# A one-core transformer tower: two layer norms share one power on GpSimd, and small operations go from GpSimd to VectorE

## The chip, the core and the metric

The kernel runs on one core of a Trainium2 chip. The metric is the device time of one execution in microseconds, the median of several runs. The core's engines are TensorE (PE, with its weight loads PEld), VectorE (DVE), ScalarE (ACT), GpSimd (POOL) and SyncE (SP), which only issues DMAs here.

## The reference

For 128 sequences of 128 tokens, three parts follow each other; D is 64.

```python
# embedding: gather, three gelus, one fused gelu, first norm
item_emb, geo, visit = emb_table[ids], geo_table[ids], visit_table[ids]
cat = concat(gelu(item_emb @ w_item + b), gelu(geo @ w_geo + b), gelu(visit @ w_visit + b))
h = item_emb + 0.1 * layer_norm(gelu(cat @ w_fuse + b_fuse), gamma, beta) * (ids != 0)
# attention, 4 heads of 16, on the second norm of h
h = h + attention(layernorm(h))
# feed-forward on the third norm x3; of each sequence's 128 tokens 63 are routed
x3 = layernorm(h)
weights = x3 @ wr + br
y = gelu_tanh(x3 @ w1 + b1) @ w2 + b2
h = h + x3 + where(selected, y * weights, 0)
```

The routing takes the 63 tokens of highest weight of each sequence. The kernel computes y for all tokens and applies the selection at the end. Each norm needs (variance + 1e-5) ** -0.5 for each token.

## The kernel before

Tokens of a sequence lie on the 128 partitions, sequences on the free axis. The 128 sequences are worked in 32 groups of four (`GB` is 4). Every engine runs the same software pipeline written by hand: a function `step(i, odd, half)` of each engine is called for i from -2 to 33, and in it a is group i+2 (embedding and first norm), b is i+1 (second norm, q, k, v), c is i (scores and softmax), e is i-1 (values and output projection) and d is i-2 (third norm and feed-forward). GpSimd's step also fetches group i+3. The first and last steps are written out; those between are a hardware loop of two steps a turn. `on(g)` says whether group g exists. Each engine works its own instructions in order and waits on semaphores counted by group.

What the change and the prediction touch:

- Each norm has statistics (`stats`, L573), an aggregation into mean and variance (`moments`, L580, tiles `mv1` to `mv3`), the reciprocal square root `rs1` to `rs3` (`rstd` on GpSimd: L352 adds epsilon, L355 is the power with `minus_half`), and a normalization on VectorE (`normalize`, L585, into `x2` and `x3`). All of `mv`, `rs` have four columns, one for each sequence of the group.
- For the first norm GpSimd multiplies `rs1` by the mask `valid` (L412); VectorE uses it in L761, which writes the state `R` (h1) from `t1`, `rs1` and `u`.
- `fetch` on GpSimd copies four columns of indices (L338) into `idx` and starts four gathers (L344) into `G`. `visit` (L373) and `base` (L361, L366) prepare the gathered rows.
- L417 and L420 on GpSimd multiply x3 by the routing weights and add x3 to R.
- L669 on VectorE takes a sequence's maximum of the scores; there are four in a step. TensorE transposes them (L961) when all are there. TensorE also transposes x2 (L953) and x3 (L980).
- L678 adds the output projection (TensorE L827) to R; TensorE waits for it in L924 of the same step.
- ScalarE's second gelu `hid` (L520) and the softmax's exponential (L527) each need a table load, as does the first gelu (L471). L478 copies the values' product and stands once in a step.

Of the kernel before, what the change touches and what calls it, by code (L numbers as in the profile page):

```python
# [32 lines left out]
ALU = mybir.AluOpType  # L33
# [11 lines left out]
GB = 4  # L45
# [33 lines left out]
def build(nc, ids, table, packed, out):  # L79
    with ExitStack() as ctx:  # L80
# [3 lines left out]
        def sem(name):  # L84
# [33 lines left out]
        rs1, rs2, rs3 = (sb(f"rs{n}", [P, GB]) for n in (1, 2, 3))  # L118
        minus_half = sb("minus_half", [P, GB])
# [53 lines left out]
            "st1_ready", "mv1_ready", "rs1_ready", "rm1_ready", "t1_ready",  # L173
            "u0_ready", "u_ready", "h1_ready", "st2_ready", "mv2_ready", "rs2_ready", "x2_ready",
# [4 lines left out]
            "h2_ready", "st3_ready", "mv3_ready", "rs3_ready", "x3_ready",   # L179
# [155 lines left out]
        def _(pool):  # L335
            def fetch(g, par):

                pool.tensor_copy(idx[par][:, :], of(idx_all, g)).then_inc(S["idx_ready"], 1)  # L338
# [64 lines left out]
            def step(i, odd, half):  # L403
                a, d, nxt = i + 2, i - 2, i + 3
                if on(d):
                    rstd(mv3, rs3, "mv3_ready", "rs3_ready", d)
                if on(nxt):
                    fetch(nxt, 1 - odd)
                if on(a):
                    rstd(mv1, rs1, "mv1_ready", "rs1_ready", a)  # L410
                    wait(pool, "rs1_ready", 2, a, alone=True)
                    pool.tensor_tensor(rs1[:, :], rs1[:, :], of(valid, a), ALU.mult  # L412
                                       ).then_inc(S["rm1_ready"], 1)
                if on(d):
# [10 lines left out]
                if on(a):  # L425
                    rstd(mv2, rs2, "mv2_ready", "rs2_ready", a)
# [110 lines left out]
        def _(dve):  # L537
# [6 lines left out]

            dve.memset(ones_r[:, :].bitcast(F32), 1.0)
            dve.wait_ge(consts_in, 16)
# [29 lines left out]
            def moments(st, mv, st_done, mv_done, g):  # L576
# [4 lines left out]
                last.then_inc(S[mv_done], 1)  # L581

# [90 lines left out]
            def step(i, odd, half):  # L673
                a, b, c, e, d = i + 2, i + 1, i, i - 1, i - 2
                if on(d):
# [5 lines left out]
                if on(b):  # L681
                    moments(st2, mv2, "st2_ready", "mv2_ready", b)
                if on(d):
                    wait(dve, "h2_ready", 1, d, alone=True)
                    stats(kept(d), st3, "st3_ready", d)
                if on(c):
                    maxima(c, (0,))
                if on(d):
                    moments(st3, mv3, "st3_ready", "mv3_ready", d)
# [4 lines left out]
                if on(b):  # L694

                    wait(dve, "rs2_ready", 2, b)
# [6 lines left out]
                if on(d):  # L703
                    wait(dve, "rs3_ready", 2, d)
# [33 lines left out]
                if on(a):  # L738

                    moments(st1, mv1, "st1_ready", "mv1_ready", a)  # L740
                    wait(dve, "mv1_ready", 1, a)
# [13 lines left out]
                if on(a):  # L755
# [3 lines left out]
                    wait(dve, "rm1_ready", 1, a)  # L759
                    for s in range(GB):  # L760
                        last = dve.scalar_tensor_tensor(kept(a)(s), t1[:, s, :], rs1[:, s:s + 1],  # L761
# [24 lines left out]
            pipeline(dve, step)  # L786
# [307 lines left out]
```

## Time and profile before

| | |
|---|---|
| median of 3 runs | 580.38 us (578.63 to 581.15) |
| profiled execution | 582.28 us, span 580.5 us |
| PE busy | 488.0 us, 84% |
| VectorE busy | 444.6 us, 77% |
| ScalarE busy | 411.6 us, 71% |
| GpSimd busy | 378.0 us, 65% |
| TensorE's granted clock, mean | 0.942 of full |

The span runs from the first to the last instruction. Busy is the time in which an engine has an instruction in work. The chain of waits is followed back from the last instruction, at each step to what released it.

### The profile page before, as it was taken

Reading aid. Unit: us, or ns where it says so; the run is one execution under the profiler, and the core shown is the slowest. Engines: PE = TensorE matmul, PEld = TensorE weight load, DVE = VectorE, ACT = ScalarE, POOL = GpSimd, SP = SyncE. Lnnn points to the kernel's source line nnn. Section 1 sums busy time; section 2 is a strip of 40 time slices with the busy share of each in tenths; the row PEclk is TensorE's granted clock in tenths of the full one; section 3 lists DMA queues with packets and bytes.
Section 4 is the critical chain, followed back from the end, with each engine's and each line's share of the span. In section 5 each row is a group of like instructions: output and inputs, shape, how many; then the busy total and the mean of one; then the engine's idle time right before and its main releaser. Section 6 shows DMA issues by size and latency. Waiting matters only on the chain.

```text
span 580.5 us, 14228 instructions
## 1 busy us (share of the span) xinstructions
PE 488.0 (84%) x4100; PEld 377.4 (65%) x4100; DVE 444.6 (77%) x1757; ACT 411.6 (71%) x694; POOL 378.0 (65%) x571
## 2 busy tenths in 40 slices
PE   0767788988999899898999999899998897988644
PEld 0445566767777677776777777677776765765443
DVE  5266667887888888778878888788887884887887
ACT  1326676788888788787787888788887774866730
POOL 6576456666777677667767677767776674442575
PEclk9879889999999999899999999999999997999855
DMA  3154444544454544545444444445454443333344
GB/s 99 21 94 114 100 104 82 101 105 106 108 110 109 112 106 103 111 90 112 99 95 100 106 105 109 107 107 112 112 107 99 99 100 66 90 92 91 76 102 116
DMA packets 89634, 57.74 MB, mean 99 GB/s; under 512 B 27408, under 2 KB 79248, under 8 KB 89488
## 3 DMA queue, kind: packets, MB, share of 16 engines
q1 hardware_dynamic: 83472, 47.55, 33.0%
q0 software_dynamic: 6144, 9.97, 11.8%
q8 instruction: 8, 0.13, 0.1%
q14 instruction: 10, 0.08, 0.1%
HBM read 11.08 MB, written 4.19 MB: 26 GB/s over the span
## 4 chain that ended last, share of the span: by engine, by line
PE 40%; ACT 16%; issue 14%; DVE 11%; POOL 9%; another core or an unknown queue 6%; DMA 2%; ACTq 0%; SPq 0%; DVEq 0%; POOLq 0%
PE psum L924 5%; POOL G L344 4%; PE psum L917 4%; PE psum L861 4%; PE psum L945 4%; ACT L520 3%; POOL rs L355 3%; PE psum L968 3%; ACT L527 3%; PE psum L943 3%; PE psum L1003 3%; PE psum L897 3%; PE psum L837 2%; PE psum L931 2%
## 5 line engine op out<-in xcount | busy, mean ns | idle before, releaser
L344 POOL DMA_INDIRECT G<-table,idx x128 | 126.6, 989 | 61.2 <-issue 58.9
L355 POOL TENSOR_TENSOR rs<-rs,minus_half 128x4 f32<-128x4 f32 x96 | 100.7, 1049 | 16.7 <-POOL rs L352 9.7
L669 DVE TENSOR_REDUCE neg_max<-psum 128x4 f32<-128x512 f32 x128 | 83.4, 674 | 0.6 <-PE psum L917 0.6
L837 PE MATMUL psum<-wt,hid 128*128 128x64 f32 x512 | 66.6, 286 | 10.1 <-ACT hid L520 10.0
L837 PEld LDWEIGHTS psum<-wt,hid 128*128 128x128 f32 x512 | 62.9, 200 | 13.4 <-ACT hid L520 13.4
L761 DVE SCALAR_TENSOR_TENSOR R<-t,rs,u 128x64 f32 (+1 forms) x128 | 52.6, 469 | 23.4 <-POOL rs L412 23.4
L352 POOL TENSOR_SCALAR rs<-mv 128x4 f32<-128x4 f32 x96 | 22.9, 238 | 72.7 <-DVE mv L580 69.0
L527 ACT ACTIVATE prob<-psum 128x512 f32<-128x512 f32 x128 | 69.7, 613 | 0.5 <-PE psum L880 0.2
L585 DVE TENSOR_SCALAR x<-R,mv,rs 128x64 f32 (+1 forms) x256 | 62.5, 308 | 4.8 <-POOL rs L355 4.8
L520 ACT ACTIVATE hid<-psum,wt 128x512 f32<-128x512 f32 x64 | 40.5, 684 | 29.7 <-remote 19.8
L724 DVE SCALAR_TENSOR_TENSOR q_s<-psum,wt,q_mask 128x512 fp32r<-128x512 f32 x32 | 24.0, 751 | 41.9 <-ACT q_mask L498 24.4
L878 PE MATMUL psum<-max_row,ones_r 128*128 128x512 f32 x128 | 54.4, 425 | 0.0
L880 PEld LDWEIGHTS psum<-q_bd,k_pair 128*128 128x128 f32 x256 | 49.2, 192 | 5.7
L880 PE MATMUL psum<-q_bd,k_pair 128*128 128x256 f32 x256 | 51.4, 282 | 0.0
L1003 PE MATMUL psum<-x3t,wt 64*128 64x256 f32 x256 | 40.6, 441 | 12.1 <-ACT x3t L505 9.4
L520 ACT ACT_TABLE_LOAD x31 | 39.8, 1283 | 6.8 <-PE psum L1003 6.3
L527 ACT ACT_TABLE_LOAD x32 | 41.1, 1283 | 3.0 <-PE psum L880 2.4
L917 PE MATMUL psum<-k_bd,q_s 128*128 128x512 f32 x128 | 40.6, 440 | 0.6 <-DMA k_bd<-k_hi 0.6
L573 DVE BATCH_NORM_STATS2 st<-R 128x6 f32 (+1 forms) x256 | 37.8, 210 | 4.1
L498 ACT ACTIVATE q_mask<-psum,bq_lo,wt 128x512 fp32r<-128x512 f32 x32 | 24.9, 777 | 21.8 <-PE psum L968 16.9
L924 PE MATMUL psum<-ig_in,wt 128*128 128x512 f32 x64 | 37.2, 664 | 2.9 <-ACT ig_in L466 1.8
L471 ACT ACT_TABLE_LOAD x30 | 38.5, 1283 | 0.5
(116 smaller groups left out, 1138.8 us busy)
## 6 DMA issues: line engine op xcount, KB each, us to landing
q_bd<-q_s SPq DMA_DIRECT2D x256, 64.0 KB
k_bd<-k_hi SPq DMA_DIRECT2D x128, 64.0 KB
k_pair<-k_hi SPq DMA_DIRECT2D x64, 128.0 KB
k_pair<-k_lo SPq DMA_DIRECT2D x64, 128.0 KB
out<-R SPq DMA_DIRECT2D x11, 256.0 KB, 3.0
G<-table,idx POOLq DMA_INDIRECT x128
wt<-packed SPq DMA_DIRECT2D x1, 1028.5 KB, 5.4
out<-R SPq DMA_DIRECT2D x2, 512.0 KB, 4.0
```

What stands on the lines that cost most here:

```text
L344: pool.indirect_dma_start(G[par][:, b, :], None, table, bass.IndirectOffsetOnAxis(ap=idx[par][:, b:b + 1], axis=0),).then_inc(gathered[par ...
L355: pool.tensor_tensor(rs[:, :], rs[:, :], minus_half[:, :], ALU.pow).then_inc(S[dst], 1)
L520: act.activation(by_row(hid[:, m, :]), two_banks((ffn_bank(d), ffn_bank(d) + 1), m), ACT.Gelu_apprx_tanh, bias=w["b_1"][:, m:m + 1]).then_ ...
L527: act.activation(prob[:, s, :, :].rearrange("p h q -> p (h q)"), bank[SCORES[s]][:, :], ACT.Exp, scale=SCALE).then_inc(S["prob_ready"], 1)
L585: last = dve.tensor_scalar(dst[:, b, :], src(b), mv[:, b, 0:1], rs[:, b:b + 1], ALU.subtract, ALU.mult)
L669: dve.tensor_reduce(neg_max[:, HEADS * s:HEADS * s + HEADS], bank[SCORES[s]][:, :].rearrange("p (h k) -> p h k", h=HEADS), AX, ALU.max, ne ...
L837: last = mm(bank[ffn_bank(d) + 1][:, s * D:(s + 1) * D], hid[:, m, slot(s)[0]], w["w_2"][:, m * D:(m + 1) * D], start=(m == 0), stop=(m == 1))
L878: mm(bank[SCORES[s]][:, :], ones_r[:, :], max_row[:, s, :], start=True, stop=False)
L880: last = mm(bank[SCORES[s]][:, pair * 2 * P:(pair + 1) * 2 * P], k_pair[odd][:, pair, tok], q_bd[odd][:, at, pair, :, :].rearrange("p h q ...
L917: mm(bank[SCORES[s]][:, :], q_s[:, tok], k_bd[:, at, :, :].rearrange("p h k -> p (h k)"), start=True, stop=True).then_inc(S["s_ready"], 1)
L924: mm(bank[6][:, :], w["w_ig"], ig_in[:, :], start=True, stop=True).then_inc(S["ig_ready"], 1)
L1003: mm(bank[ffn_bank(d) + r][:, m * 2 * P:(m + 1) * 2 * P], w["w_1"][rows, m * P:(m + 1) * P], x3t[rows, :], start=True, stop=True, tile_pos ...
```

## The change

The epsilon add goes from GpSimd to VectorE, into `moments`, for all three norms. GpSimd's two powers for the second norm of group b and the third norm of group d become one, over the eight columns of `ve23`, at the start of its step; it waits for both. The mask product and the index copy go to VectorE as well; the product gets its own tile `rm1`. On VectorE the third aggregation now stands before the first maximum. VectorE's hardware loop has one turn (two steps) fewer, since the copy reaches to group i+3.

```diff
-            def rstd(mv, rs, src, dst, g):
+            def rstd(ve, rs, src, dst, g):
                 wait(pool, src, 1, g, alone=True)
-                pool.tensor_scalar(rs[:, :], mv[:, :, 1], LN_EPS, None, ALU.add
-                                   ).then_inc(S[dst], 1)
-                wait(pool, dst, 2, g, 1, alone=True)
-                pool.tensor_tensor(rs[:, :], rs[:, :], minus_half[:, :], ALU.pow
+                pool.tensor_tensor(rs[:, :], ve[:, :], minus_half[:, 0:GB], ALU.pow
                                    ).then_inc(S[dst], 1)
...
             def step(i, odd, half):
-                a, d, nxt = i + 2, i - 2, i + 3
-                if on(d):
-                    rstd(mv3, rs3, "mv3_ready", "rs3_ready", d)
+                a, b, d, nxt = i + 2, i + 1, i - 2, i + 3
+                if on(b) or on(d):
+                    if on(b):
+                        wait(pool, "ve2_ready", 1, b, alone=True)
+                    if on(d):
+                        wait(pool, "ve3_ready", 1, d, alone=True)
+                    pool.tensor_tensor(rs23[:, :], ve23[:, :], minus_half[:, :], ALU.pow
+                                       ).then_inc(S["rs23_ready"], 1)
                 if on(nxt):
                     fetch(nxt, 1 - odd)
                 if on(a):
-                    rstd(mv1, rs1, "mv1_ready", "rs1_ready", a)
-                    wait(pool, "rs1_ready", 2, a, alone=True)
-                    pool.tensor_tensor(rs1[:, :], rs1[:, :], of(valid, a), ALU.mult
-                                       ).then_inc(S["rm1_ready"], 1)
+                    rstd(ve1, rs1, "ve1_ready", "rs1_ready", a)
...
-            def moments(st, mv, st_done, mv_done, g):
+            def moments(st, mv, ve, st_done, mv_done, ve_done, g):
...
                 last.then_inc(S[mv_done], 1)
+                wait(dve, mv_done, 1, g)
+                dve.tensor_scalar(ve[:, :], mv[:, :, 1], LN_EPS, None, ALU.add
+                                  ).then_inc(S[ve_done], 1)
...
+                if on(i + 3):
+                    dve.tensor_copy(idx[1 - odd][:, :], of(idx_all, i + 3)
+                                    ).then_inc(S["idx_ready"], 1)
...
+                    wait(dve, "rs1_ready", 1, a, alone=True)
+                    dve.tensor_tensor(rm1[:, :], rs1[:, :], of(valid, a), ALU.mult
+                                      ).then_inc(S["rm1_ready"], 1)
+                    wait(dve, "rm1_ready", 1, a, alone=True)
...
-            pipeline(dve, step)
+            pipeline(dve, step, ahead=3)
```

GpSimd before, in the last step but some that still fetches, just behind its loop. The first two rows are the third norm's, the next two the fetch, then the first norm's, and the last two the second norm's.

```order
L352 TENSOR_SCALAR rs<-mv 128x4
L355 TENSOR_TENSOR rs<-rs,minus_half 128x4
L338 COPY idx<-idx_all 128x4
L344 DMA G<-table,idx 128x152 x4
L352 TENSOR_SCALAR rs<-mv 128x4
L355 TENSOR_TENSOR rs<-rs,minus_half 128x4
L412 TENSOR_TENSOR rs<-rs,valid 128x4
L417 TENSOR_TENSOR xw<-x,wt 128x256
```

The same place in the changed kernel:

```order
L411 TENSOR_TENSOR rs<-ve,minus_half 128x8
L348 DMA G<-table,idx 128x152 x4
L356 TENSOR_TENSOR rs<-ve,minus_half 128x4
L420 TENSOR_TENSOR xw<-x,wt 128x256
L423 TENSOR_TENSOR R<-R,x 128x256
```

Of the eight instructions up to the routing product four are left, and one of the two powers is twice as wide.

VectorE before, at the start of the step behind its loop; L678 is the residual, L669 the maxima, L585 x2 and then x3:

```order
L678 TENSOR_TENSOR R<-R,psum 128x256
L580 BN_AGGR mv<-st 128x2 x4
L573 BN_STATS st<-R 128x6 x4
L669 TENSOR_REDUCE neg_max<-psum 128x4
L580 BN_AGGR mv<-st 128x2 x4
L669 TENSOR_REDUCE neg_max<-psum 128x4
```

The same place in the changed kernel:

```order
L683 COPY idx<-idx_all 128x4
L688 TENSOR_TENSOR R<-R,psum 128x256
L584 BN_AGGR mv<-st 128x2 x4
L587 TENSOR_SCALAR ve<-mv 128x4
L577 BN_STATS st<-R 128x6 x4
L584 BN_AGGR mv<-st 128x2 x4
L587 TENSOR_SCALAR ve<-mv 128x4
L676 TENSOR_REDUCE neg_max<-psum 128x4 x2
```

A copy and two epsilon adds stand before the maxima, and the third aggregation has moved ahead of both of them.

## Rows read from the trace of the kernel before

**Rows 1.** The page's chain that ended last: share of the span by engine.

```profile
PE 40%; ACT 16%; issue 14%; DVE 11%; POOL 9%; another core or an unknown queue 6%; DMA 2%; ACTq 0%; SPq 0%; DVEq 0%; POOLq 0%
```

**Rows 2.** Busy time by step: window, length, each engine, clock, DMA share, GB/s.

```profile
155.18:170.19 15.01, 14.18 (x129) 11.30 (x130) 12.59 (x53) 12.72 (x22) 10.94 (x18) 1.00 0.50 108
...
249.19:263.81 14.62, 14.14 (x129) 11.23 (x130) 11.25 (x50) 12.76 (x22) 10.30 (x16) 1.00 0.42 89
263.81:280.15 16.34, 14.45 (x129) 11.25 (x130) 13.48 (x55) 12.69 (x22) 11.79 (x19) 1.00 0.54 117
...
342.10:356.78 14.68, 14.20 (x129) 11.22 (x130) 12.27 (x51) 12.76 (x21) 10.62 (x18) 1.00 0.48 107
...
434.78:450.99 16.21, 14.69 (x129) 11.27 (x130) 11.92 (x51) 12.81 (x22) 10.36 (x17) 1.00 0.47 108
```

**Rows 3.** Timeline of ScalarE: start, duration, instruction, idle time before and releaser.

```profile
271.82 1.26 ACT L520 ACTIVATE hid<-psum,wt 128x512 f32<-128x512 f32 x2 [1.95 <-remote]
...
302.83 1.26 ACT L520 ACTIVATE hid<-psum,wt 128x512 f32<-128x512 f32 x2 [0.85 <-remote]
```

**Rows 4.** Timeline of GpSimd, from one index copy to the next.

```profile
152.48 0.23 POOL L352 TENSOR_SCALAR rs<-mv 128x4 f32<-128x4 f32 x1 [0.44 <-DVE mv L580]
...
155.32 0.19 POOL L338 COPY idx<-idx_all 128x4 int32 x1
...
170.47 0.19 POOL L338 COPY idx<-idx_all 128x4 int32 x1
```

**Rows 5.** GpSimd's groups by shape: busy us, mean ns, then idle before.

```profile
L355 POOL TENSOR_TENSOR rs<-rs,minus_half 128x4 f32<-128x4 f32 x96 | 100.7, 1049 | 16.7 <-POOL rs L352 9.7 <-issue 5.0
L366 POOL TENSOR_TENSOR u<-u,G 128x256 f32<-128x256 f32 x32 | 23.4, 731 | 5.0 <-POOL u L361 4.4
...
L352 POOL TENSOR_SCALAR rs<-mv 128x4 f32<-128x4 f32 x96 | 22.9, 238 | 72.7 <-DVE mv L580 69.0 <-issue 3.0
...
L412 POOL TENSOR_TENSOR rs<-rs,valid 128x4 f32<-128x4 f32 x32 | 6.5, 202 | 6.0 <-POOL rs L355 5.1 <-issue 0.3
...
L338 POOL COPY idx<-idx_all 128x4 int32 x24 | 4.5, 186 | 0.0
```

**Rows 6.** Timeline of all engines in the step at 272 to 282 us.

```profile
272.76 1.76 DVE L761 SCALAR_TENSOR_TENSOR R<-t,rs,u 128x64 f32 x4 [0.44 <-POOL rs L412]
...
276.22 0.42 DVE L678 TENSOR_TENSOR R<-R,psum 128x256 f32 x1 [0.30 <-PE psum L827]
276.56 0.37 DVE L580 BATCH_NORM_AGGREGATE mv<-st 128x2 f32<-128x6 f32 x4
...
277.13 0.23 POOL L352 TENSOR_SCALAR rs<-mv 128x4 f32<-128x4 f32 x1 [0.84 <-DVE mv L580]
...
278.79 0.98 DVE L585 TENSOR_SCALAR x<-R,mv,rs 128x64 f32 x4
...
279.68 1.28 DVE L669 TENSOR_REDUCE neg_max<-psum 128x4 f32<-128x512 f32 x2
...
281.41 0.38 PE L953 MATMUL psum<-wt,x 128*128 128x128 f32 x2
...
282.06 0.27 PE L961 MATMUL psum<-wt,neg_max 128*128 128x128 f32 x1
```

**Rows 7.** Instructions that write or read `room`: duration min, median, max in ns.

```profile
L629 DVE TENSOR_SCALAR room<-room x2: 142/148/154, 540.1 to 571.6; 112x1 f32<-112x1 f32 x1, 16x1 f32<-16x1 f32 x1
```

**Rows 8.** Timeline of VectorE in the first steps, and GpSimd beside L761 later.

```profile
24.86 0.87 DVE L761 SCALAR_TENSOR_TENSOR R<-t,rs,u 128x64 f32<-128x64 f32 x4 [0.97 <-POOL rs L412]
...
272.63 0.73 POOL L417 TENSOR_TENSOR xw<-x,wt 128x256 f32<-128x256 f32 x1
273.31 0.73 POOL L420 TENSOR_TENSOR R<-R,x 128x256 f32 x1
```

**Rows 9.** The chain of waits in the head: start, duration, what.

```profile
28.51 0.19 POOL idx L338
...
28.97 1.13 POOL G L344
```

**Rows 10.** Timeline of GpSimd in the tail.

```profile
547.05 0.57 POOL L352 TENSOR_SCALAR rs<-mv 128x4 f32<-128x4 f32 x1 [0.67 <-DVE mv L580]
547.71 1.45 POOL L355 TENSOR_TENSOR rs<-rs,minus_half 128x4 f32<-128x4 f32 x1
```

More of the change, by code:

```diff
@@ L117, in build @@
         mv1, mv2, mv3 = (sb(f"mv{n}", [P, GB, 2]) for n in (1, 2, 3))
-        rs1, rs2, rs3 = (sb(f"rs{n}", [P, GB]) for n in (1, 2, 3))
-        minus_half = sb("minus_half", [P, GB])
+        ve1, rs1 = sb("ve1", [P, GB]), sb("rs1", [P, GB])
+        ve23, rs23 = sb("ve23", [P, 2 * GB]), sb("rs23", [P, 2 * GB])
+        ve2, ve3 = ve23[:, 0:GB], ve23[:, GB:2 * GB]
+        rs2, rs3 = rs23[:, 0:GB], rs23[:, GB:2 * GB]
+        rm1 = sb("rm1", [P, GB])
+        minus_half = sb("minus_half", [P, 2 * GB])
         t1 = sb("t1", [P, GB, D])
@@ L172, in build @@
             "cat_ready", "catv_ready", "fu_ready", "fused_ready", "ft_ready",
-            "st1_ready", "mv1_ready", "rs1_ready", "rm1_ready", "t1_ready",
-            "u0_ready", "u_ready", "h1_ready", "st2_ready", "mv2_ready", "rs2_ready", "x2_ready",
+            "st1_ready", "mv1_ready", "ve1_ready", "rs1_ready", "rm1_ready", "t1_ready",
+            "u0_ready", "u_ready", "h1_ready", "st2_ready", "mv2_ready",
+            "ve2_ready", "rs23_ready", "x2_ready",
             "xt_ready", "x2t_ready", "q_ready", "k_ready", "v_ready",
@@ L178, in build @@
             "prob_ready", "pv_ready", "pvt_out", "pb_ready", "rsum_ready", "o_ready", "ot_ready", "o_t_ready", "wo_ready",
-            "h2_ready", "st3_ready", "mv3_ready", "rs3_ready", "x3_ready",
+            "h2_ready", "st3_ready", "mv3_ready", "ve3_ready", "x3_ready",
             "xw_ready", "w_ready", "r_ready", "x3t_ready", "x3t_out", "f1_ready",
@@ L336, in fetch @@
             def fetch(g, par):
-                pool.tensor_copy(idx[par][:, :], of(idx_all, g)).then_inc(S["idx_ready"], 1)
                 wait(pool, "idx_ready", 1, g, alone=True)
@@ L424, in step @@
                     base(nxt, 1 - odd)
-                if on(a):
-                    rstd(mv2, rs2, "mv2_ready", "rs2_ready", a)
                 if type(i) is int and i >= NG - 1:
@@ L543, in _ @@
                               ).then_inc(ids_ready, 1)
+            dve.wait_ge(ids_ready, 2)
+            dve.tensor_copy(idx[0][:, :], of(idx_all, 0)).then_inc(S["idx_ready"], 1)
             dve.memset(ones_r[:, :].bitcast(F32), 1.0)
+            dve.memset(ve23[:, :], 1.0)
             dve.wait_ge(consts_in, 16)
@@ L681, in step @@
                 if on(b):
-                    moments(st2, mv2, "st2_ready", "mv2_ready", b)
+                    moments(st2, mv2, ve2, "st2_ready", "mv2_ready", "ve2_ready", b)
                 if on(d):
@@ L685, in step @@
                     stats(kept(d), st3, "st3_ready", d)
+                if on(d):
+                    moments(st3, mv3, ve3, "st3_ready", "mv3_ready", "ve3_ready", d)
                 if on(c):
                     maxima(c, (0,))
-                if on(d):
-                    moments(st3, mv3, "st3_ready", "mv3_ready", d)
                 if on(c):
@@ L694, in step @@
                 if on(b):
-                    wait(dve, "rs2_ready", 2, b)
+                    dve.wait_ge(S["rs23_ready"], i + 2)
                     ends(dve, "xt_ready", 1, b - 1)
@@ L703, in step @@
                 if on(d):
-                    wait(dve, "rs3_ready", 2, d)
+                    dve.wait_ge(S["rs23_ready"], i + 2)
                     ends(dve, "r_ready", 1, d - 1)
@@ L738, in step @@
                 if on(a):
-                    moments(st1, mv1, "st1_ready", "mv1_ready", a)
-                    wait(dve, "mv1_ready", 1, a)
+                    moments(st1, mv1, ve1, "st1_ready", "mv1_ready", "ve1_ready", a)
                     for s in range(GB):
@@ L758, in step @@
                     ends(dve, "u_ready", 1, a)
-                    wait(dve, "rm1_ready", 1, a)
+                    wait(dve, "rs1_ready", 1, a, alone=True)
+                    dve.tensor_tensor(rm1[:, :], rs1[:, :], of(valid, a), ALU.mult
+                                      ).then_inc(S["rm1_ready"], 1)
+                    wait(dve, "rm1_ready", 1, a, alone=True)
                     for s in range(GB):
-                        last = dve.scalar_tensor_tensor(kept(a)(s), t1[:, s, :], rs1[:, s:s + 1],
+                        last = dve.scalar_tensor_tensor(kept(a)(s), t1[:, s, :], rm1[:, s:s + 1],
                                                         u[:, s, :], ALU.mult, ALU.add)
```

## The prediction, written before the changed kernel had run

> **What bounds the kernel now.** I read the chain of waits first, then the step times, then the engines inside one step. One step of the software pipeline lasts about 15.5 us, and 36 of them make the span. Over the whole span the chain lies on TensorE for 40% and ScalarE for 16%, on VectorE for 11% and GpSimd for 9% [rows 1]. So the two engines that the change touches hold a fifth of it, and the question is where.
>
> Counting from one ScalarE copy of the values (L478) to the next, the steps at full clock are of three kinds [rows 2]. The shortest take 14.62 to 14.71 us (three steps; two are shown). Others take 15.2 to 16.4 us with the same TensorE and ScalarE work: in these ScalarE has loaded the table of the second gelu and then waits 0.85 to 1.95 us for something that the profile can't name [rows 3]. In both kinds the chain runs through TensorE and ScalarE alone. The third kind, three steps from 140 to 185 us and four from 389 to 451 us, has the chain on GpSimd and VectorE. There the loop is: two powers, index copy, four gathers, the first norm's power, the mask product, VectorE's residual and its statistics, and back. From one index copy to the next it takes 15.15 us [rows 4]. The seven last 107.2 us together, 15.3 each; the first and the last row of [rows 2] are two of them.
>
> **The change, part by part, in one step.** GpSimd loses three epsilon adds (0.238 us each, and about 0.19 us until the power behind it starts), one of three powers (1.04 to 1.05 us), the index copy (0.186) and the mask product (0.202, with about 0.19 ahead of it) [rows 5]. Together 3 x 0.42 + 1.04 + 0.19 + 0.39 = 2.9 us of its loop. The two powers that remain are one of 4 columns and one of 8.
>
> *The power over 8 columns* isn't in the trace. Below, it costs what 4 columns cost, 1.05 us. Above, all but the price of a small operation grows with the columns: the mask product over the same 4 columns takes 0.20, so (1.05 - 0.20) x 2 + 0.20 = 1.9 us [rows 5]. An add over 256 columns takes 0.731 us, 2.1 ns a column beyond that 0.20; the power's 0.85 us over 4 columns is 100 times as much a column, so either a power has a long fixed part or it is slow per column. The rows don't decide. I take 1.3 us, nearer to the lower end, since a hundredfold price for a column is the odder of the two. The Trainium skill (GPSIMD Engine Reference, section 3.1) puts an elementwise operation at about 2.6 cycles an element beyond its dispatch; by that alone the four extra columns would be free, and the add's row agrees with it while the power's row can't be explained by it.
>
> *VectorE gains* three epsilon adds, the mask product and the index copy. The nearest row is the scalar add on one column, 0.142 to 0.154 us [rows 7]; with the wait for the aggregation in front I take 0.2 us for each of the four, 0.1 for the copy: 0.9 us a step. VectorE is busy 12.6 of 15.0 us in a step of the third kind [rows 2], so it still fits. The copy stands where it waited for the output projection (0.30 us idle) [rows 6], the first norm's epsilon stands ahead of the wait for that norm's power (0.44 us). Those two are hidden. What isn't hidden stands between the residual (L678) and the fourth maximum: epsilon two, epsilon three, and the third aggregation, which now has to wait for statistics with no maximum between (0.05). That is 0.45 us.
>
> *The wait on the shared power.* It starts 0.2 us after epsilon three, as the epsilon add on GpSimd (277.13) started 0.2 us after the aggregation that runs between the residual and the statistics, ended at 276.93 [rows 6]. VectorE has two maxima (1.25 us) until it needs the result for x2. With a power of 1.05 us the result is there at 0.2 + 1.05 + 0.15 = 1.4 us: a 0.15 us wait. Queued behind it are x2, maxima three and four, x3. So the fourth maximum ends 0.45 + 0.15 = 0.6 us later than now, 281.56 instead of 280.96. TensorE comes to the transpose of the maxima at 282.06 and to that of x2 at 281.41; x2, which now starts at 278.79 and takes 0.98, would end at 280.4 [rows 6]. So 0.5 us are left, and **a shared power over about 1.55 us stalls TensorE in every step**. At my 1.3 us it doesn't.
>
> *GpSimd's loop afterwards.* 15.15 - 2.9, plus 0.45 for VectorE's part of it, 0.2 for the mask product there, 0.25 for the wider power: 13.2 us (13.8 at 1.9 us). That is below 14.65, so the loop stops being a bound. The seven steps could fall to the shortest kind: 107.2 - 7 x 14.65 = 4.6 us. The unnamed wait follows right behind most of the short steps (14.62 is followed by 16.34) [rows 2], so I book half: 2.3 us.
>
> *Head and tail.* In the head the chain goes twice through epsilon, power, index copy and gather, [rows 9]; copy to gather is 0.46 us there and most of it goes, 0.1 us of each epsilon too, less 0.25 for the wider power: 0.3 to 0.5 us each, 0.8 together. In the tail the third norm's power is twice on the chain, at 1.45 us with 0.66 for the epsilon before it [rows 10]; the epsilon becomes 0.2 on VectorE, the power grows by some 0.25, though its second half is not needed there: 0.2 us each, 0.4. That gives 2.3 + 0.8 + 0.4 = 3.5 us, and with GpSimd's gathers beginning about a microsecond earlier in some steps where TensorE waits for them, 4 us.
>
> *The shared port.* The residual of the first norm has two SBUF inputs. Alone, in the first steps, its four instructions take 0.87 us; in the loop, where GpSimd's product and add of 0.73 us each run beside them, 1.76 [rows 6, 8]. The mask product on VectorE has two SBUF inputs too, and GpSimd now goes from the power straight into those two. It may lose up to their 1.45 us, where the residual already loses 0.9 of it. I put h1 at 0.2 us later after the power, against a power that begins 0.35 us earlier: nothing. The Trainium skill (SBUF — State Buffer, section "SBUF: two separate sides") calls that port pair an exclusive lock for the whole instruction; by it the residual gains nothing from a shorter chain, and the trace agrees as far as 1.76 against 0.87 goes.
>
> **Rivals.** *Power by the column (slower).* At 1.9 us the fourth maximum is late by 1.9 - 1.55 = 0.35 us in some 28 steps, 9.8 us. Each head and tail pass is 0.6 us worse than above, 4 x 0.6 = 2.4. Against it stand the third kind's steps, which still lose 0.3 each, 2 us, and the part of the stall that the unnamed wait takes in, perhaps 4. Result 580.4 + 6 = 586 us, up to 589. It decides from 1.55 us on. For it speaks the 0.85 us over 4 columns; against it nothing but that oddity.
>
> *The time moves into the unnamed wait (no change).* The six steps from 263.81 to 356.78 us have a mean of 15.50 us, though they vary from 14.7 to 16.3 [rows 2]. If something sets that mean, the seven steps gain nothing on balance and head and tail give 1 us: 580 us. For it speaks that each of the four steps under 14.95 us was followed by one of 16.3 us or more.
>
> *VectorE becomes the bound.* 12.6 + 0.9 = 13.5 us of work in 14.65; with its waits for ScalarE's q mask it would be about full. It would show as 14.9 us steps: about 578 us. I count it with the first case.
>
> **How the numbers follow.** The span of the profiled execution is 580.5 us, its own time 582.3, the median of the runs 580.4; I subtract the 4 us from the median, 576.4. A no-change measurement of this kernel is told apart at about 0.5%, 2.9 us. Chances: forecast 0.50 (of it faster 0.75, same 0.20, slower 0.05), power by the column 0.30 (0.05, 0.20, 0.75), unnamed wait 0.20 (0.10, 0.75, 0.15). That makes 0.41 faster, 0.31 same, 0.28 slower. The range goes from 570 (the seven steps at 14.65 in full, and half of what the gathers or the unnamed wait could give besides) to 589 (power by the column). The likeliest case's own range is 571 to 580.
>
> **What the changed profile would show.** The 128x8 power's mean says at once which case it is: under 1.55 or over. The chain should be free of GpSimd between 100 and 480 us, the seven steps near 14.7. VectorE's group of normalizations should wait for the shared power by 0.1 to 0.3 us a step, and TensorE's transpose of the maxima for VectorE not at all. If that transpose waits, I am wrong on the power or on the 0.45 us. If the steps keep a mean of 15.5 us with GpSimd idle, the unnamed wait is the bound.

## The result, and the profile after

The changed kernel takes 598.17 us (median of 4 runs, 596.51 to 601.43) against 580.76 us for the kernel before (4 runs on the same chip). The ratio is 1.032, with a 95% interval of 1.026 to 1.038: **slower by 3%, where 576.4 us were forecast, and above the range's 589**. Some runs of the kernel before and of about half of the others were disturbed: ratios leave them out, so they are not exactly the ratio of the medians, and kernels whose profile is of such a run carry a * in the table below.

The page of the changed kernel: busy time of each engine, the chain that ended last by engine, and GpSimd's two groups of powers (busy us, mean ns, idle before and its releaser).

```profile
PE 488.4 (82%) x4100; PEld 370.0 (62%) x4100; DVE 470.6 (79%) x1918; ACT 414.7 (70%) x694; POOL 334.0 (56%) x382
...
DVE 42%; issue 24%; POOL 20%; PE 5%; another core or an unknown queue 2%; DVEq 2%; DMA 1%; ACT 1%; POOLq 0%; ACTq 0%; SPq 0%
...
L411 POOL TENSOR_TENSOR rs<-ve,minus_half 128x8 f32<-128x8 f32 x35 | 58.7, 1678 | 83.1 <-DVE ve L587 82.8
...
L356 POOL TENSOR_TENSOR rs<-ve,minus_half 128x4 f32<-128x4 f32 x32 | 33.2, 1037 | 88.3 <-DVE ve L587 87.7
```

The groups of VectorE's moved operations, by shape (busy us, mean ns, idle before and its releaser):

```profile
L587 DVE TENSOR_SCALAR ve<-mv 128x4 f32<-128x4 f32 x96 | 17.1, 179 | 3.3
L769 DVE TENSOR_TENSOR rm<-rs,valid 128x4 f32<-128x4 f32 x32 | 13.3, 416 | 12.1 <-POOL rs L356 12.0
L683 DVE COPY idx<-idx_all 128x4 int32 x24 | 11.3, 472 | 0.0
```

The chain was 40% on TensorE and 11% on VectorE [rows 1]; now VectorE has 42%, GpSimd 20% and TensorE 5%. GpSimd is busy 44 us less and yet its share of the chain has doubled. The wide power takes 1.68 us, which is 0.64 more than one over four columns and 0.4 less than two of them.

One step of the changed kernel's loop on VectorE: start, duration, instruction, idle time before it and its releaser.

```profile
283.35 0.50 DVE L683 COPY idx<-idx_all 128x4 int32 x1
283.76 0.41 DVE L688 TENSOR_TENSOR R<-R,psum 128x256 f32 x1
...
285.80 0.17 DVE L587 TENSOR_SCALAR ve<-mv 128x4 f32<-128x4 f32 x1
285.88 1.28 DVE L676 TENSOR_REDUCE neg_max<-psum 128x4 f32<-128x512 f32 x2
287.85 1.19 DVE L592 TENSOR_SCALAR x<-R,mv,rs 128x64 f32 x4 [0.69 <-POOL rs L411]
288.80 1.28 DVE L676 TENSOR_REDUCE neg_max<-psum 128x4 f32<-128x512 f32 x2
...
291.98 0.75 DVE L734 SCALAR_TENSOR_TENSOR q_s<-psum,wt,q_mask 128x512 fp32r<-128x512 f32 x1 [0.39 <-issue]
...
295.95 0.40 DVE L769 TENSOR_TENSOR rm<-rs,valid 128x4 f32<-128x4 f32 x1 [0.47 <-POOL rs L356]
296.60 1.10 DVE L773 SCALAR_TENSOR_TENSOR R<-t,rm,u 128x64 f32 x4 [0.25 <-DVE rm L769]
```

The same step on GpSimd:

```profile
283.09 0.73 POOL L367 TENSOR_TENSOR u<-u,G 128x256 f32<-128x256 f32 x1 [0.18 <-POOL u L362]
...
286.16 1.66 POOL L411 TENSOR_TENSOR rs<-ve,minus_half 128x8 f32<-128x8 f32 x1 [2.34 <-DVE ve L587]
287.98 1.07 POOL L348 DMA_INDIRECT G<-table,idx  x1 [0.17 <-issue]
...
294.58 1.04 POOL L356 TENSOR_TENSOR rs<-ve,minus_half 128x4 f32<-128x4 f32 x1 [1.77 <-DVE ve L587]
295.61 0.72 POOL L420 TENSOR_TENSOR xw<-x,wt 128x256 f32<-128x256 f32 x1
```

And on TensorE, where it takes the maxima:

```profile
290.13 0.33 PE L973 MATMUL psum<-wt,neg_max 128*128 128x128 f32 x1 [0.16 <-DVE neg_max L676]
```

GpSimd stands idle for VectorE twice in the step, 2.34 and 1.77 us. It has stopped being a bound as forecast, but VectorE now stands idle for both of its powers: 0.69 us before x2, and 0.47 before the mask product. From the start of the residual (283.76) to the end of the fourth maximum (288.80 + 1.28 = 290.08) it takes 6.32 us. Before it was 280.96 - 276.22 = 4.74 [rows 6], so the fourth maximum comes 1.58 us later, not 0.6.

Busy time in two steps that follow each other (window, length, then PE, PEld, DVE, ACT, POOL, granted clock, DMA share, GB/s):

```profile
269.75:286.93 17.18, 14.62 (x129) 11.06 (x130) 13.65 (x58) 12.82 (x21) 9.54 (x12) 1.00 0.50 99
286.93:302.62 15.69, 14.47 (x129) 11.19 (x130) 13.47 (x58) 12.82 (x21) 9.56 (x12) 1.00 0.49 99
```

Through the whole loop steps of 15.7 us and steps of 17.2 us take turns, at full clock and with the same work. What tells them apart is one wait that the trace can't name, in front of the statistics of the first norm in each long step:

```profile
275.00 0.75 DVE L734 SCALAR_TENSOR_TENSOR q_s<-psum,wt,q_mask 128x512 fp32r<-128x512 f32 x1 [0.50 <-issue]
276.96 0.63 DVE L577 BATCH_NORM_STATS2 st<-psum 128x6 f32<-128x64 f32 x4 [1.21 <-remote]
```

The 18 steps of the loop's middle (the eighth to the twenty-fifth) have a mean of 16.48 us, against 15.60 in the profile before. 18 x 0.88 = 15.8 us is the whole difference of the spans, 594.7 - 580.5 = 14.2, and more. The loss is in the loop, not in head or tail.

### The profile page after: what moved, and what is told of

The parts are those of the page before. It is cut to its first block, busy times and chain, and to the rows that moved or that the text cites. A ratio compares the mean times of both kernels' runs of the same rounds, so it can differ in the third digit from the quotient of the medians.

```text
span 594.7 us, 14007 instructions
## 1 busy us (share of the span) xinstructions
PE 488.4 (82%) x4100; PEld 370.0 (62%) x4100; DVE 470.6 (79%) x1918; ACT 414.7 (70%) x694; POOL 334.0 (56%) x382
## 4 chain that ended last, share of the span: by engine, by line
DVE 42%; issue 24%; POOL 20%; PE 5%; another core or an unknown queue 2%; DVEq 2%; DMA 1%; ACT 1%; POOLq 0%; ACTq 0%; SPq 0%
POOL rs L411 8%; DVE x L592 7%; DVE st L577 7%; POOL rs L356 5%; DVE neg_max L676 5%; DVE mv L584 5%; DVE R L773 4%; POOL G L348 4%; DVE rm L769 2%; DVE ve L587 2%; DVE q_s L734 2%; DVE R L688 2%; PE psum L849 1%; DVE Y L667 1%
## 5 line engine op out<-in xcount | busy, mean ns | idle before, releaser
L348 POOL DMA_INDIRECT G<-table,idx x128 | 125.2, 978 | 39.3 <-issue 35.6
L411 POOL TENSOR_TENSOR rs<-ve,minus_half 128x8 f32<-128x8 f32 x35 | 58.7, 1678 | 83.1 <-DVE ve L587 82.8
L592 DVE TENSOR_SCALAR x<-R,mv,rs 128x64 f32 (+1 forms) x256 | 67.0, 324 | 25.1 <-POOL rs L411 24.7
L356 POOL TENSOR_TENSOR rs<-ve,minus_half 128x4 f32<-128x4 f32 x32 | 33.2, 1037 | 88.3 <-DVE ve L587 87.7
L676 DVE TENSOR_REDUCE neg_max<-psum 128x4 f32<-128x512 f32 x128 | 81.9, 681 | 0.0
L577 DVE BATCH_NORM_STATS2 st<-R 128x6 f32 (+1 forms) x256 | 39.3, 216 | 3.9
L1015 PEld LDWEIGHTS psum<-x3t,wt 64*128 64x128 f32 x256 | 23.4, 197 | 27.5 <-issue 17.2
L773 DVE SCALAR_TENSOR_TENSOR R<-t,rm,u 128x64 f32 (+1 forms) x128 | 35.1, 332 | 6.1 <-DVE rm L769 5.8
L929 PE MATMUL psum<-k_bd,q_s 128*128 128x512 f32 x128 | 38.5, 421 | 1.4 <-DMA k_bd<-k_hi 1.3
L584 DVE BATCH_NORM_AGGREGATE mv<-st 128x2 f32<-128x6 f32 x384 | 36.1, 155 | 4.0 <-issue 0.2
```

What stands on the lines that cost most here:

```text
L348: pool.indirect_dma_start(G[par][:, b, :], None, table, bass.IndirectOffsetOnAxis(ap=idx[par][:, b:b + 1], axis=0),).then_inc(gathered[par ...
L356: pool.tensor_tensor(rs[:, :], ve[:, :], minus_half[:, 0:GB], ALU.pow).then_inc(S[dst], 1)
L411: pool.tensor_tensor(rs23[:, :], ve23[:, :], minus_half[:, :], ALU.pow).then_inc(S["rs23_ready"], 1)
L577: last = dve.bn_stats(st[:, b, :], src(b))
L584: last = dve.bn_aggr(mv[:, b, :], st[:, b, :])
L592: last = dve.tensor_scalar(dst[:, b, :], src(b), mv[:, b, 0:1], rs[:, b:b + 1], ALU.subtract, ALU.mult)
```

## The experiments

There were eighteen runs in five sets, some of them of the same kernel again; the kernels of a set share a chip and the runs of the kernel before. Chips differ as much as the kernels do: in the runs that the ratios use, the kernel before has a median of 580.5, 559.7, 580.8, 581.6 and 578.7 us in sets 1 to 5 (3 and 5 are the same chip). So only ratios within a set are compared. "Step" is the mean of the same 18 loop steps in the run's profile; "unnamed" is the time in them that ScalarE and VectorE together waited for what the trace can't name.

| set | kernel | median us | ratio to before (95%) | step us | unnamed us |
|---|---|---|---|---|---|
| | before | 580.76 | 1 | 15.60 | 17.9 |
| | changed | 598.17 | 1.032 (1.026 to 1.038) | 16.48 | 11.0 |
| 1 | shared power alone | 597.78 | 1.023 (1.012 to 1.034) | 16.27 | 0 |
| 1 | index copy alone * | 575.17 | 0.987 (0.981 to 0.992) | 15.50 | 1.4 |
| 1 | mask product alone * | 589.40 | 1.003 (0.994 to 1.011) | 16.77 | 53.2 |
| 1 | epsilon alone | 579.70 | 0.987 (0.981 to 0.994) | 15.81 | 11.6 |
| 2 | changed, powers apart | 553.74 | 0.989 (0.986 to 0.992) | 14.98 | 0 |
| 2 | changed, joint wait, two powers | 560.02 | 0.998 (0.995 to 1.001) | 15.16 | 0 |
| 2 | index copy and epsilon | 556.37 | 0.994 (0.991 to 0.997) | 15.02 | 0 |
| 2 | before, with powers of other widths in the set-up | 610.45 (one run) | none | 15.28 | 0 |
| 3 | changed | 597.26 | 1.030 (1.025 to 1.035) | 16.41 | 9.8 |
| 3 | shared power alone | 595.19 | 1.027 (1.021 to 1.033) | 16.22 | 0 |
| 3 | changed, powers apart | 589.04 | 1.001 (0.996 to 1.007) | 15.73 | 11.6 |
| 3 | the same, index copy in the gap * | 603.17 | 1.029 (1.020 to 1.038) | 16.26 | 21.6 |
| 4 | changed | 600.26 | 1.037 (1.030 to 1.043) | 16.49 | 11.2 |
| 4 | changed, joint wait, two powers | 569.77 | 0.981 (0.976 to 0.986) | 15.16 | 0 |
| 4 | changed, x2 behind all maxima | 596.53 | 1.027 (1.023 to 1.032) | 16.44 | 15.7 |
| 4 | powers apart, index copy in the gap | 610.05 | 1.049 (1.042 to 1.057) | 16.42 | 24.9 |
| 5 | changed | 598.78 | 1.035 (1.021 to 1.050) | 16.48 | 11.2 |
| 5 | changed, joint wait, two powers * | 568.68 | 0.981 (0.966 to 0.996) | 15.19 | 1.4 |

**One part at a time (set 1).** First the shared power on its own, with the epsilons left on GpSimd:

```diff
 # before, GpSimd
-                if on(d):
-                    rstd(mv3, rs3, "mv3_ready", "rs3_ready", d)
+                    if on(b):
+                        wait(pool, "mv2_ready", 1, b, alone=True)
+                        pool.tensor_scalar(ve2, mv2[:, :, 1], LN_EPS, None, ALU.add
+                                           ).then_inc(S["ve2_ready"], 1)
...
+                    pool.tensor_tensor(rs23[:, :], ve23[:, :], minus_half[:, :], ALU.pow
+                                       ).then_inc(S["rs23_ready"], 1)
```

> The kernel before with only the shared power: epsilon adds, mask product and index copy stay on GpSimd, both epsilon adds stand before one power over 8 columns at the start of the step. Theory A (the wide power is most of the loss: the changed kernel shows 1.66 us for 8 columns against 1.04 for 4, so x2 gets its factors late): x2 waits 0.5 to 0.9 us a step, +1.0 to +2% (587 to 592 us). Theory B (the small operations on VectorE are most of it): the shared power saves GpSimd 0.4 us a step and is harmless, 577 to 584 us.

It loses 2.3% alone. Its waits (engine, line, releaser: us in total, times, longest):

```profile
DVE x L599 <- POOL rs L421: 57.9, 34, 2.4
...
PEld psum L967 <- DVE x L599: 28.5, 27, 3.5
```

VectorE waits 57.9 / 34 = 1.7 us each time, and TensorE's transpose of x2 stands behind it in 27 of the steps. That is more than the 0.5 to 0.9 us expected, and more than in the changed kernel: here the two epsilon adds still stand on GpSimd ahead of the power. The unnamed wait is absent from this kernel's loop, so its loss owes nothing to it.

The index copy alone (the copy as in the change, with `ahead=3`):

> The kernel before with only the index copy on VectorE (and VectorE's loop one turn shorter). Theory A: hidden, within 0.5% of 580.8, or faster by up to 4 us since GpSimd's gathers begin earlier. Theory B: the copy takes 0.47 us where GpSimd runs beside it, instead of 0.19, and delays the residual for TensorE: +3 to +8 us.

It gains 1.3%, where 0.7% was the most expected. On GpSimd the first gather starts 0.18 us behind the third norm's power:

```profile
285.70 1.04 POOL L354 TENSOR_TENSOR rs<-rs,minus_half 128x4 f32<-128x4 f32 x1 [0.18 <-POOL rs L351]
286.92 1.11 POOL L343 DMA_INDIRECT G<-table,idx  x1 [0.18 <-issue]
```

In the kernel before, the copy stood between the two, and with it an idle time of 1.1 to 1.2 us ahead of the first gather in every loop step, for which the trace names no cause:

```profile
154.32 1.04 POOL L355 TENSOR_TENSOR rs<-rs,minus_half 128x4 f32<-128x4 f32 x1 [0.18 <-POOL rs L352]
155.32 0.19 POOL L338 COPY idx<-idx_all 128x4 int32 x1
156.62 1.12 POOL L344 DMA_INDIRECT G<-table,idx  x1 [1.12 <-issue]
```

From the end of the power to the gather it was 156.62 - 155.36 = 1.26 us. So the copy's move takes 1.1 us a step from GpSimd, and not the 0.19 us that the prediction counted.

On VectorE the copy takes 470 ns, not the 0.1 us of the forecast, in a place where VectorE waited 0.30 us anyway [rows 6].

The mask product alone, and the epsilon adds alone (the edits of the change's `moments` and `rstd`, each norm with its own power):

> The kernel before with only the mask product on VectorE. Theory A: within 0.5%. Theory B: product 0.42 us plus about 0.25 of waits against 0.20 plus 0.19 on GpSimd, so the residual of the first norm comes 0.2 to 0.4 us later in the steps where GpSimd's loop sets the pace: 0 to +5 us.

> The kernel before with only the three epsilon adds on VectorE, powers of 4 columns each where they were. Theory A: faster, since 3 x 0.42 us leave GpSimd's loop and 0.2 us each come to VectorE: 575 to 579 us. Theory B: VectorE's part of the loop grows by as much as GpSimd's shrinks: 580 to 586 us.

The mask product changes nothing measurable; its profile has 53 us of unnamed waits in the loop, so nothing is read from its steps. The epsilon adds take 0.19 us each on VectorE and gain 1.3%, a little more than the 0.3 to 1.0% expected. So three of the four moves are neutral or good and the shared power is bad.

**Powers apart, or only joined in their wait (set 2).** The changed kernel with one power for each norm again, at its old place:

```diff
-                    pool.tensor_tensor(rs23[:, :], ve23[:, :], minus_half[:, :], ALU.pow
-                                       ).then_inc(S["rs23_ready"], 1)
+                if on(d):
+                    rstd(ve3, rs3, "ve3_ready", "rs3_ready", d)
...
+                if on(a):
+                    rstd(ve2, rs2, "ve2_ready", "rs2_ready", a)
```

> The changed kernel with the shared power undone: two powers of 4 columns, each where it stood before; epsilon, mask product and index copy stay on VectorE. Theory A (the shared power is the whole loss; alone it cost 2.3%, while index copy and epsilon alone gained 1.3% each and the mask product nothing): 2 to 2.6% below the kernel before. Theory B (the moved operations together overfill VectorE): within 1% of before, though each alone was harmless.

And the joint wait kept, but two powers of four columns behind it, that of the second norm first, each with a signal of its own:

```diff
-                    pool.tensor_tensor(rs23[:, :], ve23[:, :], minus_half[:, :], ALU.pow
-                                       ).then_inc(S["rs23_ready"], 1)
+                    if on(b):
+                        pool.tensor_tensor(rs2, ve2, minus_half[:, 0:GB], ALU.pow
+                                           ).then_inc(S["rs2_ready"], 1)
+                    if on(d):
+                        pool.tensor_tensor(rs3, ve3, minus_half[:, 0:GB], ALU.pow
+                                           ).then_inc(S["rs3_ready"], 1)
```

> The changed kernel with its joint wait for both epsilons, but two powers of 4 columns behind it, the second norm's first. Theory A1 (the 0.62 us that the wide power is longer is the loss): x2 gets its factors 0.6 us earlier than in the changed kernel; 583 to 590 us. Theory A2 (the later start, behind the third norm's epsilon, is the larger part): 592 to 598 us, as the changed kernel.

> The kernel before with index copy and epsilon adds on VectorE, mask product on GpSimd, powers apart. If the two gains add: 2.6% below before, 566 us. If both only shorten the same GpSimd loop until TensorE and ScalarE are the bound: 1.3 to 2% below. Against the unshared kernel it shows the mask product again: equal if that is worth nothing.

Apart, the moves gain 1.1%, and index copy and epsilon alone 0.6%. With the joint wait the kernel is level with before. None of the three came out as expected: the first was to gain 2 to 2.6% or to be within 1% of before, the second to lose at least 0.4%, the third to gain 1.3 to 2.6%. VectorE with the powers apart starts x2 without a wait:

```profile
280.74 1.29 DVE L673 TENSOR_REDUCE neg_max<-psum 128x4 f32<-128x512 f32 x2
281.94 0.98 DVE L589 TENSOR_SCALAR x<-R,mv,rs 128x64 f32 x4
282.83 1.28 DVE L673 TENSOR_REDUCE neg_max<-psum 128x4 f32<-128x512 f32 x2
```

**What a power costs by its width (set 2).** The kernel before with 28 more instructions on GpSimd in the set-up, powers and products over 1 to 64 columns:

```diff
+            for n in (1, 2, 4, 8, 16, 32, 64):
+                for op in (ALU.pow, ALU.mult):
+                    for k in range(2):
+                        pool.tensor_tensor(scr_c[:, at:at + n], scr_a[:, 0:n], scr_b[:, 0:n], op)
```

> The kernel before with 28 more GpSimd operations in its set-up: powers and products over 1, 2, 4, 8, 16, 32 and 64 columns, twice each, into columns that nothing reads. From 1.04 us for 4 columns and 1.66 for 8: a line of 0.42 us plus 0.155 a column, so 0.58 for 1 and 10.3 us for 64. If the power works in blocks: steps instead. Products: 0.20 us and some 2 ns a column.

Each group below holds two powers and two products; its one time was 610.45 us, with the added work.

```profile
L389 POOL TENSOR_TENSOR scr_c<-scr_a,scr_b 128x64 f32<-128x64 f32 x4 | 21.6, 5421 | 0.0
...
L389 POOL TENSOR_TENSOR scr_c<-scr_a,scr_b 128x8 f32<-128x8 f32 x4 | 3.6, 910 | 0.0
L389 POOL TENSOR_TENSOR scr_c<-scr_a,scr_b 128x4 f32<-128x4 f32 x4 | 2.3, 594 | 0.0
```

The shortest of the 28 took 183 ns, the longest 10,535. If a product takes 0.2 us at 4 and 8 columns, as in [rows 5], a power takes 2 x 0.594 - 0.2 = 0.99 us at 4 columns, 1.62 at 8, and the longest is 10.54 at 64. From 4 to 64 that is 9.55 / 60 = 0.16 us a column on a fixed 0.35 us, close to the line expected; from 4 to 8 columns it is 0.16 too. A power costs some 75 times as much a column as the add over 256 columns (2.1 ns [rows 5]). The Trainium skill (GPSIMD Engine Reference, section 3.1) gives about 2.6 cycles an element for a `tensor_tensor`, by its 1.2 GHz an estimate of 2.2 ns. The add's row agrees with that, and the powers do not.

The loop of this kernel is the loop of the kernel before, and it ran on the chip of set 2 without an unnamed wait. Its steps are steady there: 15.12 us in the mean of 17, the eighteenth 18.0. The page's chain by engine:

```profile
POOL 32%; issue 21%; DVE 19%; PE 14%; SPq 3%; ACT 3%; DMA 3%; POOLq 1%; DVEq 1%; ACTq 0%
```

So on that chip the kernel before runs at the loop of GpSimd and VectorE, for which the prediction read 15.15 us [rows 4], and TensorE and ScalarE do not hold the chain as they do in [rows 1]. With that loop shortened and the powers apart the step is 14.98 us: there the moved operations were worth 0.14 us a step.

**The changed kernel again, and the index copy in a gap (set 3).** In the last of the four the powers are apart and the index copy is issued for group i+4, right ahead of VectorE's wait for the queries:

```diff
-                if on(i + 3):
-                    dve.tensor_copy(idx[1 - odd][:, :], of(idx_all, i + 3)
-                                    ).then_inc(S["idx_ready"], 1)
...
+                if on(i + 4):
+                    dve.wait_ge(gathered[odd], (half + 1) * 64 + 64)
+                    dve.tensor_copy(idx[odd][:, :], of(idx_all, i + 4)
+                                    ).then_inc(S["idx_ready"], 1)
```

> The changed kernel once more, so that the next three stand beside it on one chip. Theory (VectorE and the two powers stand in series, the shared power of 1.68 us is the longer of them): 3 to 4% slower than before, the wait of VectorE's x for the shared power 0.6 to 0.8 us per step. Rival (the loss belongs to the unnamed waits of the chip on which it was profiled first): under 1% slower here if those waits are absent.

> The kernel before with the shared power alone. Theory: 2 to 3.5% slower than before, since the shared power of 1.69 us is waited for by VectorE 1.7 us per step. Rival (the moves to VectorE are what costs): within 0.5% of before.

> The changed kernel with the two powers of four columns each kept apart. Theory: 1 to 1.5% faster than before, so 4 to 5% faster than the changed kernel. Rival (VectorE's added small operations are the loss): slower than before.

> As the one with the powers apart, with the index copy issued four groups ahead, right before VectorE's wait for the queries, where VectorE has a gap, and away from GpSimd's residual add. Theory (VectorE is the bound once the powers are apart, and the copy's 0.47 us is mostly the port shared with GpSimd): the copy falls to about 0.2 us and the kernel is 0.5 to 1.5% faster than with the powers apart alone. Rival (the copy lay in time that nothing waited for): same within 0.3%.

The loss of the changed kernel (3.0%) comes back, and that of the shared power alone (2.7%) does so on a second chip. Two forecasts failed. With the powers apart the kernel is level with before here, not 1.1% faster: its steps are 14.9 us with others of 16.4 between them. And the index copy in the gap is 2.9% slower, though the copy itself did what was expected, 176 ns instead of 422, and VectorE waits for nothing in front of it:

```profile
L726 DVE COPY idx<-idx_all 128x4 int32 (+1 forms) x30 | 5.3, 176 | 0.0
```

**Length or start of the power (set 4).** In the third kernel x2 is normalized behind all four maxima:

```diff
+                if on(c):
+                    maxima(c, (2, 3))
...
-                if on(c):
-                    maxima(c, (2, 3))
```

> The changed kernel beside the next three on one chip. Theory (VectorE and the powers stand in series): 3 to 4% slower than before on any chip, since the loop has no unnamed wait in it. Rival (the loss is in the unnamed waits): under 1.5% slower on a chip without them.

> The changed kernel with the joint wait kept but with two powers of four columns. If the power's length is what costs: within 1% of before and 2 to 3% faster than the changed kernel. If the joint wait costs as much: 1.5 to 2.5% slower than before.

> The changed kernel with x2 normalized behind maxima three and four, so that the 1.68 us power has 2.5 us of maxima beside it. Theory (what costs is that VectorE stands idle for the power): the wait falls from 0.7 us per step to under 0.1, the steps get 0.5 to 0.7 us shorter and the kernel is 1 to 3% faster than the changed one. Rival (TensorE needs x2's transpose early): the wait moves to TensorE's transpose of x2, no faster than the changed kernel.

> Powers apart, index copy four groups ahead in VectorE's gap before the queries, where it took 0.18 us instead of 0.42. On a chip with unnamed waits: 2 to 3% slower than before, as measured. On a chip without them: 0.8 to 1.6% faster than before if the added work on VectorE no longer counts, and no better than the one with the powers apart (1.1% faster) if TensorE is the bound.

The joint wait with two narrow powers is 1.9% faster than before and 569.77 / 600.26 = 0.949 of the changed kernel, more than either expectation allowed. All that differs from the changed kernel is that one power over eight columns became two over four, the second norm's first and with a signal of its own. Its step on this chip is the 15.16 us that it has on the fast chip of set 2, and no unnamed wait stands in it. On GpSimd the second norm's power ends at 318.49, before VectorE comes to x2 at 318.67:

```profile
317.46 1.03 POOL L412 TENSOR_TENSOR rs<-ve,minus_half 128x4 f32<-128x4 f32 x1 [2.36 <-DVE ve L591]
318.46 1.01 POOL L415 TENSOR_TENSOR rs<-ve,minus_half 128x4 f32<-128x4 f32 x1
...
318.67 0.98 DVE L596 TENSOR_SCALAR x<-R,mv,rs 128x64 f32 x4
```

Moving x2 takes the wait for the power away (3.4 us in the whole run) and moves it on, as the rival had it: TensorE now waits 0.95 us for x2, and the queries are 0.87 us late. The short step falls from 15.68 only to 15.52 us, and the kernel is within 1% of the changed one:

```profile
323.31 0.44 PE L965 MATMUL psum<-wt,x 128*128 128x128 f32 x2 [0.95 <-DVE x L592]
...
325.82 0.75 DVE L734 SCALAR_TENSOR_TENSOR q_s<-psum,wt,q_mask 128x512 fp32r<-128x512 f32 x1 [0.87 <-ACT q_mask L499]
```

The index copy in the gap is slower than before again, by 4.9% where 2 to 3% were expected, and its ratio is the highest of all. Its steps swing between 14.5 and 19.2 us, its chain lies on TensorE for 61%, and VectorE waits 43.7 us for ScalarE's q mask. The page's chain by engine:

```profile
PE 61%; issue 10%; another core or an unknown queue 9%; ACT 6%; DVE 6%; POOL 6%; DMA 1%; SPq 0%; ACTq 0%; POOLq 0%; DVEq 0%
```

The waits:

```profile
DVE q_s L733 <- ACT q_mask L496: 43.7, 23, 4.7
```

**Once more (set 5).**

> The changed kernel once more. On a chip without unnamed waits the steps are all 15.68 us against some 15.0 before, 24 x 0.7 = 16 us: about 3% slower. On a chip with them every other step is 17.2 us, as before: 3 to 4% slower. If the loss is under 1.5% on a chip without them, the theory that the wide power stands in VectorE's loop is wrong.

> Joint wait, two powers of four columns: steps of 15.0 to 15.3 us on any chip, so 0 to 0.5% faster than before on a chip without unnamed waits and about 2% faster on one with them; 3 to 5% faster than the changed kernel either way.

The chip was that of set 3, so a chip without unnamed waits was not had for the changed kernel. The two give 1.035 and 0.981 again.

## Why the prediction was wrong

**The step that failed** is the wait on the shared power, in two of its terms. *The power over 8 columns* was taken as 1.3 us of 1.05 to 1.9; it takes 1.68. The choice was argued from the oddity of a power being a hundred times as slow a column as an add. It is 75 times as slow a column. The rows of the kernel before [rows 5] left open how much of a power is fixed, and the choice between the two was a guess. The prediction's threshold was about 1.55 us, and the result lies on the far side of it, as the rival "power by the column" (30%, 586 us, up to 589) had it.

*The time ahead of the fourth maximum* was given 0.6 us, with a power of 1.05 us; by the same working it is 0.85 at the 1.3 us chosen, which the prediction does not write out. It is 1.58. The wait is 0.69 us, where that working gives 0.40 at 1.3 us and 0.78 at 1.68: it held, and the power's price failed in it. x2 would start 0.83 us later even without the wait (3.40 us behind the residual's start against 2.57 [rows 6]), where 0.45 was booked. The remaining 0.06 lies between x2's start and the end of the maxima. Before, TensorE came to the maxima 282.06 - 280.96 = 1.10 us behind the fourth [rows 6]. The 1.58 us are 0.48 more than that, and TensorE takes the maxima 290.13 - 283.76 = 6.37 us behind the residual's start, not 282.06 - 276.22 = 5.84.

**Why it cost more than the rival's 586.** The rival priced TensorE's stall, 0.35 us a step at a power of 1.9 us; at the measured 1.68 it would be 1.68 - 1.55 = 0.13. So the rival had the power right and the price of it too low. VectorE became the loop, the third rival, which I had counted with the forecast at 578 us because 13.5 us of work "still fits". The work was right: 13.47 us in the step of 15.69. In part that was luck. The five moved operations take 3 x 0.18 + 0.42 + 0.47 = 1.4 us a step and not 0.9, and the residual of the first norm gives 0.66 back, as told below. What I left out is that VectorE works in order and stands idle within its loop: 0.69 for the shared power, 0.39 for the queries, 0.47 and 0.25 around the mask product, 1.8 us together, which with 13.47 and small gaps makes 15.69. With the powers apart the first falls away and the step is 14.98 us on the chip of set 2, the 14.9 of that rival. The idle time by itself is not the price, though: with x2 behind all maxima the wait for the power goes, and the step falls by 0.16 us only, since x2's transpose and the queries then come late (set 4). What costs is that x2 comes late.

**By parts** (the fence is VectorE's timeline in the first steps of the changed kernel). The epsilon adds at 0.2 us: 0.179. The copy at 0.1: 0.472 in the loop. The mask product at 0.2: 0.416, and 0.25 until the residual starts. Both run beside an operation of GpSimd with two inputs, and both took 0.16 us in the first steps, where none ran beside them:

```profile
24.97 0.16 DVE L769 TENSOR_TENSOR rm<-rs,valid 128x4 f32<-128x4 f32 x1 [0.50 <-POOL rs L356]
25.17 0.87 DVE L773 SCALAR_TENSOR_TENSOR R<-t,rm,u 128x64 f32<-128x64 f32 x4
...
26.59 0.16 DVE L683 COPY idx<-idx_all 128x4 int32<-128x4 int32 x1
```

In the step shown above the copy ends at 283.85 and the mask product at 296.35, just behind the operations of GpSimd beside them, which end at 283.82 and 296.33. The Trainium skill (SBUF — State Buffer, section "SBUF: two separate sides") calls the port pair of the two engines an exclusive lock. The trace agrees: 0.16 us alone, 0.42 and 0.47 beside GpSimd, and an end with GpSimd's. The mask product now takes the block, and the four instructions of the residual behind it fell from 1.76 us [rows 6] to 1.10. The prediction had h1 0.2 us later behind the power; it comes 0.31 us earlier. From the end of the first norm's power to the end of that residual it is 297.70 - 295.62 = 2.08 us. Before it was 2.39, from this power's end, 272.13, to 274.52 [rows 6]:

```profile
271.09 1.04 POOL L355 TENSOR_TENSOR rs<-rs,minus_half 128x4 f32<-128x4 f32 x1 [0.18 <-issue]
```

GpSimd's loop lost more than the 2.9 us counted, since the index copy's 0.19 us stood for 1.1. It stopped being the bound, as said, and gave nothing, since another had taken its place. Head and tail (1.2 us of gain) are not seen. The changed kernel's first copy of the values stands at 60.8 us against 58.8, most of it an unnamed wait of 5.40 us against 3.53, but the gelu ahead of that wait starts at 54.97 against 54.84, no earlier either. From the last copy to the end it is 34.7 us against 34.8.

**The unnamed wait.** The rival that it takes the gain in is right for one thing: every second step of the changed kernel's loop holds it, 1.2 us each, in all four of its profiles (but for one step in one of them). It is not the cause of the sign. The shared power alone has none of it in its loop and loses 2.3 and 2.7%; the short steps without it are 15.68 us, where the kernel with two narrow powers needs 15.16 on either chip. How much of the changed kernel's 3% would be left on a chip without such waits was not measured. The kernel before has steps of 15.12 us without them (the run of the widths), so an estimate is 15.68 - 15.12 = 0.56 us a step, in 24 steps 13 us or 2.4% of 559.7. What causes them, why every second step, and why a kernel that swings freely on TensorE (the index copy in the gap) has more of them, stays open. That the powers apart gained 1.1% on one chip and nothing on another goes with them, but this is argued and not shown.

**A version that beats both kernels** came out of this: the changed kernel with its joint wait and two narrow powers, 0.981 in two sets and 0.998 in a third; with the powers apart it is 0.989 and 1.001.

## What to carry to other kernels

Price an unseen width of a known instruction by the row that separates fixed from per-column cost, and take the odd answer seriously when two rows of one engine differ a hundredfold. Joining two operations makes the first result as late as the second: if the consumer of the first is the one in a hurry, issue two instructions behind one wait instead. Price an operation that you move by all the time that goes with it, and not by its busy time: the index copy was busy for 0.19 us and stood for 1.1. And an engine that works in order doesn't "fit" by its busy time: add the waits that stay inside its loop, and ask which it can't do without.

## What was not expected of the hardware

The kernel before took 559.7 us on one chip and 578.7 to 581.6 on three others, 3.4 to 3.9% more (medians of the runs that the ratios use), with a granted clock of 0.949 to 0.964 on the first and 0.926 to 0.959 on the others; the unnamed waits were in profiles on the latter only. A kernel held at a steady 15.16 us by its GpSimd and VectorE kept that step on both kinds of chip, while one that ran at 14.98 us on the first had 15.73 on another. A small copy of 4 columns took 0.16 to 0.18 us alone and 0.47 to 0.50 beside GpSimd. On GpSimd the index copy in the loop was followed by 1.1 to 1.2 us of idle time before the first gather, and by 0.28 in the first steps, outside the loop; with the copy on VectorE it was 0.17 in both.
